# Dividing by exp(-ln) and a Newton step in a time mix, with the opening in another order

## The chip, the cores and the metric

One core of a Trainium2 chip runs one program; seven other cores are idle. The metric is the device time of that program in microseconds, the median of the runs of one kernel. The engines are TensorE (PE), VectorE (DVE), ScalarE (ACT), GpSimd (POOL), and the queue of DMA orders on SyncE (SP). Each engine works through its own instructions strictly in the order in which the program lists them; between engines, only semaphores order the work.

## The reference

Two layers of a gated model over x (16 sequences, 128 tokens, 256 channels) and a context of the same shape. Each layer is an attention-like part and a feed-forward part, each added to x through a gate `tanh(g)`:

```python
x = x + tanh(g_xattn[0]) * wkv(time_decay, time_first, layernorm(x), ctx)   # the time mix
x = x + tanh(g_ffn[0])   * ffn0(layernorm(x))       # gate/up/down MLP of 1024 and product-key experts
x = x + tanh(g_xattn[1]) * linear_attention(layernorm(x), ctx)
x = x + tanh(g_ffn[1])   * ffn1(layernorm(x))       # 8 routed experts, top 2, and a shared one
```

The change is in the first line. Freed of its running maximum, the time mix is, per channel and over the tokens t of a sequence, with w = exp(-exp(time_decay)) and u = time_first:

```python
den_t = past_den + exp(u + k_t);            num_t = past_num + exp(u + k_t) * v_t
y_t = num_t / den_t
past_den = w * past_den + exp(k_t);         past_num = w * past_num + exp(k_t) * v_t
```

## The kernel before, in words

**Tiling.** The 16 sequences are handled as four groups of four (GT = 4), so that a group has 512 tokens. Activations of a group are kept transposed: 256 channels are two chunks (c = 0, 1) of 128 partitions, and a chunk is 128x512. The first layer's time mix is done by group g of `WKV_FIRST`, the feed-forwards by group f of `MAIN_FIRST`.

**One written order.** There is no planner at run time. `SCHED` is a list of steps (kind, group, part), made of `START`, of the feed-forward units with the steps that `PLAN` hangs behind each, and of `LAST`. Every engine runs through the same list and issues what it has to do in each step, so the list sets the order within each engine's queue. A feed-forward has 12 units (8 of gate and up, 4 of experts); part p of `mlp` is unit p-1, and the down matmuls follow three units later. TensorE writes into six PSUM banks, taken in turn; a bank is taken again only when its reader has freed it.

**The time mix of a group**, in steps: `wkv_in` 0 moments of x (VectorE; the reciprocal root on GpSimd, L1620 or L1625); 1 normalize (VectorE L1240, or ScalarE L1023 for the steps in `NORM_ACT`); 2 TensorE transposes (L649), ScalarE takes exp into the denominator rows (L1033), and GpSimd (parts 3 and 4; VectorE for the very first) multiplies by the context, v (L531). `wkv_out` 0 and 1: for each chunk VectorE scans the denominator and then the numerator (L1276). Parts 2 and 4: ScalarE scales the numerator's own term by exp(u) (L1039), GpSimd adds the past (L1649). The denominator's own term is treated so too in groups 0 and 1 (`DEN_SCALE`: L1009, L1644) and by one VectorE operation in groups 2 and 3 (L548). Parts 2 to 5: VectorE takes the reciprocal in two halves of 256 columns (L1288); parts 3 and 5: GpSimd multiplies (L1655). Parts 6 and 7: TensorE transposes back (L770), VectorE adds to x (L1244). `x_stats` follows with the new moments, and then `mlp_in`, whose normalize for feed-forward 0 is ScalarE's.

**Around it.** `kv_k` (TensorE L781) projects a tile of the context for the second layer's attention; `kv_e` (ScalarE L1047 to L1052: two relus, a copy, an exp) makes the keys; `kv_v` (TensorE L793) multiplies keys by values; `kv_c` (ScalarE L1056) copies the sum. `split` makes the high and low parts of a weight block (ScalarE L977, GpSimd L1590) and asks SP for the block two further on. `wq` does that for the query weights, `query` uses them. `mlp` is on TensorE L654 to L656 and L678, Silu on ScalarE (L1137), the product with up on VectorE (L1414). `peer_in` brings the routing tables over (VectorE L1385 for the low part), which TensorE spreads (L744).

ScalarE computes functions from a table; where the next function is not in the table that is loaded, the program has an ACT_TABLE_LOAD in front of it.

The lines that the change replaces, with who waits for whom:

```python
        else:                                   # VectorE, wkv_out 2 to 5
            c, half = divmod(part - 2, 2)
            den = by_token(ee_a[c][:, 1, :])[:, half * GT // 2:(half + 1) * GT // 2, :]
            ...
            last = dve.reciprocal(den, den)
            if half:
                last.then_inc(recip_ready, 1)
```

Of the kernel before, what the change touches and what calls it, by code (L numbers as in the profile page):

```python
# [256 lines left out]
def build(nc, io):  # L257
    with ExitStack() as ctx:
# [204 lines left out]
        scanned = sem("scanned")  # L463
# [2 lines left out]
        recip_ready = sem("recip_ready")
# [1399 lines left out]
```

## Time and profile before

| | us |
|---|---|
| median of 3 runs | 507.49 (507.08 to 510.03) |
| the profiled execution | 508.22, of which the span 506.4 |
| TensorE busy | 450.3 (89%) |
| VectorE busy | 347.2 (69%) |
| ScalarE busy | 247.2 (49%) |
| GpSimd busy | 173.8 (34%) |

The granted TensorE clock is 0.974 of full speed in the mean. The span is from the first instruction to the last; what lies around it is the difference to the program's own time. Busy times count only work: not waits, not branches or DMA orders. An engine's idle time costs something only where the end waits for it, so the table says that TensorE is near its bound over the whole, and the stretches and timelines must say where it is not.

### The profile page before, as it was taken

How to read it: one execution, taken by the hardware profiler on the slowest of the kernel's cores; microseconds unless marked ns; L12 is line 12 of the kernel's file. 1: busy time of each engine (PE TensorE's matmuls, PEld its weight loads, DVE VectorE, ACT ScalarE, POOL GpSimd, SP SyncE). 2: the span in 40 equal slices, each digit the busy share in tenths (PEclk: the TensorE clock that was granted, in tenths of full speed). 3: DMA queues.
4: the chain of work that ended last, by engine and by line, in shares of the span. 5: the costliest groups of instructions: out<-in, count | busy, mean ns of one | idle time of the engine just before them, and what ended most of it. 6: DMA issues, size and time to landing. Idle time of an engine off the chain costs nothing. (4 is left out here: it accounts for less than half of the span.)

```text
span 506.4 us, 7287 instructions
## 1 busy us (share of the span) xinstructions
PE 450.3 (89%) x2162; PEld 356.1 (70%) x2162; DVE 347.2 (69%) x994; ACT 247.2 (49%) x479; POOL 173.8 (34%) x181
## 2 busy tenths in 40 slices
PE   2769799589989999999999998998998899899991
PEld 1447588458668776888778786887776688788860
DVE  6968569988486964577978967888778354621173
ACT  2868264223577377455044416360751544955540
POOL 3787232354022333400000000060525015477771
PEclk9999799789999999999999999999999899999997
DMA  8421212002000000980000000142323223346494
GB/s 306 164 80 57 62 33 80 5 20 83 1 1 2 0 1 0 293 218 0 1 2 1 0 2 0 32 136 74 119 71 112 88 79 111 105 150 191 123 380 138
DMA packets 32966, 42.02 MB, mean 83 GB/s; under 512 B 3483, under 2 KB 26781, under 8 KB 32928
## 3 DMA queue, kind: packets, MB, share of 16 engines
q1 hardware_dynamic: 28224, 32.28, 21.0%
q0 software_dynamic: 3744, 8.42, 4.5%
q10 hardware_dynamic: 960, 0.86, 0.5%
q8 instruction: 19, 0.31, 0.3%
q14 instruction: 19, 0.16, 0.1%
HBM read 24.97 MB, written 18.39 MB: 86 GB/s over the span
## 5 line engine op out<-in xcount | busy, mean ns | idle before, releaser
L678 PE MATMUL acc<-w_down,act_s 128*128 128x256 f32 x384 | 91.5, 384 | 0.9 <-DVE act_s L1410 0.9
L678 PEld LDWEIGHTS acc<-w_down,act_s 128*128 128x128 f32 x384 | 73.6, 193 | 12.8 <-DVE act_s L1410 1.3
L654 PE MATMUL ring<-xt_h,up_l 128*128 128x512 f32 x160 | 71.1, 444 | 1.4 <-DVE kv_sum L1490 1.4
L1137 ACT ACTIVATE act_s<-ring 128x512 f32<-128x512 f32 x48 | 28.6, 596 | 73.5 <-PE ring L656 73.3
L655 PE MATMUL ring<-xt_l,up_h 128*128 128x512 f32 x160 | 63.4, 396 | 0.0
L656 PE MATMUL ring<-xt_h,up_h 128*128 128x512 f32 x160 | 63.3, 395 | 0.0
L1625 POOL TENSOR_TENSOR rstd<-var_eps,minus_half 128x4 f32<-128x4 f32 x14 | 14.5, 1039 | 135.7 <-DVE var_eps L1225 135.7
L717 PE MATMUL ring<-up_e,act_s 128*128 x184 | 45.7, 392 | 2.3 <-issue 2.0
L1677 POOL DMA_INDIRECT x_rows<-main_a,slots x32 | 31.1, 972 | 43.7 <-ACT main_a L1158 34.8
L1414 DVE TENSOR_TENSOR act_s<-ring,act_s 128x512 f32<-128x512 f32 x32 | 21.9, 686 | 34.3 <-ACT act_s L1137 16.4
L717 PEld LDWEIGHTS ring<-up_e,act_s 128*128 128x128 f32 x184 | 34.2, 196 | 7.2 <-issue 3.2
L654 PEld LDWEIGHTS ring<-xt_h,up_l 128*128 128x128 f32 x160 | 30.6, 191 | 9.3 <-issue 2.0
L649 PE MATMUL ring<-small,xn 128*128 128x128 f32 x144 | 20.7, 290 | 18.5 <-DVE xn L1240 13.6
L655 PEld LDWEIGHTS ring<-xt_l,up_h 128*128 128x128 f32 x160 | 30.5, 190 | 7.5 <-issue 1.9
L656 PEld LDWEIGHTS ring<-xt_h,up_h 128*128 128x128 f32 x160 | 30.2, 189 | 7.2
L649 PEld LDWEIGHTS ring<-small,xn 128*128 128x128 f32 x144 | 17.5, 149 | 22.0 <-issue 9.3
L1685 POOL DMA_INDIRECT y_rows<-act_s,block_home x16 | 16.3, 1019 | 31.7 <-ACT act_s L1195 27.1
L1218 DVE BATCH_NORM_STATS2 stats<-x_nat 128x6 f32<-128x256 f32 x64 | 22.4, 412 | 4.5 <-DMA x_nat<-in_x 4.2
L1244 DVE SCALAR_TENSOR_TENSOR x_nat<-ring,small,x_nat 128x512 f32<-128x512 f32 x24 | 18.0, 749 | 10.1 <-PE ring L918 7.7
L1137 ACT ACT_TABLE_LOAD x18 | 23.1, 1283 | 0.3
L1567 DVE TENSOR_TENSOR pairs<-ring,pairs 128x256 f32<-128x256 f32 x12 | 5.1, 424 | 25.4 <-ACT pairs L1178 25.4
L1288 DVE RECIPROCAL main_a<-main_a 128x256 f32<-128x256 f32 x12 | 20.0, 1715 | 0.1
(281 smaller groups left out, 1009.6 us busy)
## 6 DMA issues: line engine op xcount, KB each, us to landing
main_b<-x_rows SPq DMA_DIRECT2D x22, 257.0 KB, 3.0
x_rows<-v_t SPq DMA_DIRECT2D x1, 3983.5 KB, 16.1
up_l<-y_rows SPq DMA_DIRECT2D x5, 512.0 KB, 5.9
stage<-in_w_mlp SPq DMA_DIRECT2D x8, 256.0 KB, 2.6
up_e<-in_w_moe SPq DMA_DIRECT2D x8, 256.0 KB, 2.6
x_rows<-v_t SPq DMA_DIRECT2D x1, 1927.5 KB, 22.4
x_nat<-in_x SPq DMA_DIRECT2D x7, 256.0 KB, 7.9
out_x<-x_nat SPq DMA_DIRECT2D x6, 256.0 KB, 5.0
```

The costliest lines, as they stand in the source:

```text
L649: last = pe.transpose(bank[:, t * P:(t + 1) * P], xn[n % 2][:, t, c * P:(c + 1) * P], ident)
L654: pe.matmul(out, wl, xh, start=first, stop=False, skip_group_check=True)
L655: pe.matmul(out, wh, xl, start=False, stop=False, skip_group_check=True)
L656: return pe.matmul(out, wh, xh, start=False, stop=final, skip_group_check=True)
L678: last = pe.matmul(acc[t // 2][:, t % 2, :], act_s[n % RING][:, tok], w_down[:, u, :], start=u == 0 and t % 2 == 0, stop=final, skip_group ...
L717: last = pe.matmul(bank[:, j * 2 * P:(j + 1) * 2 * P], x_block_t[n % 2][:, c, j * P:(j + 1) * P], up_e[:, bass.ds(e * UP + c * 2 * P, 2 * ...
L1137: act.activation(act_s[n % RING][:, :], bank[:, :], ACT.Silu).then_inc(free_sem((step, "A", u)), 1)
L1218: last = dve.bn_stats(stats[:, n, t, :], x_nat[:, b, :])
L1244: return dve.scalar_tensor_tensor(out, bank, gates[:, gate:gate + 1], out, ALU.mult, ALU.add)
L1288: last = dve.reciprocal(den, den)
L1414: free((step, "B", u), dve.tensor_tensor(s[:, :], bank[:, :], s[:, :], ALU.mult))
L1677: pool.indirect_dma_start(x_rows[group_of(g)], bass.IndirectOffsetOnAxis(ap=slots[:, t, k:k + 1], axis=0), to_send[n % SENDS], None).then_ ...
```

## The change

A group's `wkv_out` is written anew. Denominators of both chunks are scanned first (part 0), the numerators after them (part 1). ScalarE scales the own term of both denominators and GpSimd adds the past, in all groups (part 2). The quotient is then made of a guess and one Newton step: ScalarE computes `guess = exp(-ln(den))` (part 3); VectorE multiplies `den * guess`, GpSimd `num * guess`; VectorE computes `(den * guess - 2) * (num * guess)`, which is the quotient with its sign turned (part 5). The sign is taken back by the gate, whose tanh is taken of -g. In part 4 the numerator's own term and past are added: by ScalarE and GpSimd as before, for group 0 by one VectorE operation (`NUM_DVE`).

`START` and the plans of feed-forwards 0 and 1 are reordered, and the normalize of group 2 goes from VectorE to ScalarE.

```diff
-START = """wkv_in 0 0, setup 0 0, wkv_in 0 1, wkv_in 1 0, wkv_in 0 2, kv_k 0 0, kv_e 0 0, wkv_out 0 0, wkv_in 1 1, kv_k 0 1,
-    wkv_out 0 1, wkv_in 1 2, wkv_out 0 2, kv_e 0 1, kv_v 0 0, kv_c 0 0, wkv_out 0 3 4, kv_k 0 2, kv_e 0 2, wkv_in 1 3,
-    wkv_out 0 5, kv_v 0 1, kv_c 0 1, wkv_in 1 4, split 0 0, kv_k 0 3, kv_e 0 3, kv_v 0 2, kv_c 0 2, wkv_out 1 0,
-    wkv_out 0 6 7, kv_k 1 0, kv_e 1 0, kv_v 0 3, kv_c 0 3, x_stats 0 0, split 0 1, wkv_out 1 1, kv_k 1 1, kv_e 1 1, kv_v 1 0,
-    kv_c 1 0, mlp_in 0 0 1, mlp_in 0 2, kv_v 1 1, kv_k 1 2, wq 0 0, wkv_out 1 2, kv_c 1 1, kv_e 1 2, wkv_out 1 3 4"""
+START = """wkv_in 0 0, setup 0 0, wkv_in 0 1, wkv_in 0 2, wkv_in 1 0, kv_k 0 0 1, wkv_out 0 0 2, wkv_out 0 1, kv_k 0 2, wkv_out 0 3 4,
+    wkv_in 1 1, wkv_out 0 5, kv_e 0 0, wkv_in 1 2, kv_e 0 1, kv_v 0 0, kv_c 0 0, kv_e 0 2, wkv_in 1 3 4, split 0 0, wkv_out 0 6 7,
+    kv_v 0 1, kv_c 0 1, kv_k 0 3, kv_e 0 3, x_stats 0 0, kv_v 0 2, kv_c 0 2, kv_k 1 0, wkv_out 1 0, kv_e 1 0, kv_v 0 3, kv_c 0 3,
+    split 0 1, wkv_out 1 1, kv_k 1 1, kv_v 1 0, kv_c 1 0, mlp_in 0 0 1, mlp_in 0 2, kv_k 1 2, kv_e 1 1, wkv_out 1 2, kv_v 1 1, kv_c 1 1,
+    kv_e 1 2, wkv_out 1 3 4, wq 0 0"""
 PLAN = {
     ("mlp", 0): {
-        3: "route_in 2 1, route_in 2 2, query 2 0, wkv_in 2 0",
-        4: "query 2 1, wkv_in 2 1, route 0 2 3, wkv_in 2 2 3 4",
+        3: "kv_k 1 3, route_in 2 1, route_in 2 2, kv_e 1 3, query 2 0, wkv_in 2 0",
+        4: "query 2 1, wkv_in 2 1, route 0 2 3, wkv_in 2 2 3 4, kv_v 1 3, kv_c 1 3",
...
-        7: "wkv_out 2 1",
-        8: "peer_in 0 0, wkv_out 2 2 3",
-        9: "wkv_out 2 4 5",
-        10: "wkv_out 2 6 7, x_stats 2 0, kv_k 1 3, kv_e 1 3",
-        11: "mlp_in 1 0, kv_v 1 3, kv_c 1 3, kv_m 0 0 1 2 3",
+        7: "wkv_out 2 2",
+        8: "peer_in 0 0, wkv_out 2 1, kv_k 2 0 1",
+        9: "wkv_out 2 3 4 5, kv_e 2 0 1",
+        10: "wkv_out 2 6 7, x_stats 2 0, kv_v 2 0 1, kv_c 2 0 1",
+        11: "mlp_in 1 0, kv_m 0 0 1 2 3",
...
     ("mlp", 1): {
-        1: "mlp_out 0 0, route 1 4, kv_k 2 0, kv_e 2 0",
-        2: "route 1 5, kv_k 2 1, kv_v 2 0, kv_c 2 0, kv_e 2 1",
-        3: "route 1 6, wkv_in 3 0, kv_k 2 2, kv_v 2 1, kv_c 2 1, kv_e 2 2",
-        4: "route 1 7, wkv_in 3 1, kv_k 2 3, kv_v 2 2, kv_c 2 2, kv_e 2 3",
-        5: "wkv_in 3 2 3 4, route 1 8, kv_v 2 3, kv_c 2 3",
-        6: "wkv_out 3 0 1",
-        7: "wkv_out 3 2 3",
-        8: "peer_in 1 0, wkv_out 3 4 5, query 1 0",
+        1: "mlp_out 0 0, route 1 4",
+        2: "route 1 5, kv_k 2 2, kv_e 2 2",
+        3: "route 1 6, wkv_in 3 0, kv_k 2 3, kv_v 2 2, kv_c 2 2, kv_e 2 3",
+        4: "route 1 7, wkv_in 3 1, kv_v 2 3, kv_c 2 3",
+        5: "wkv_in 3 2 3 4, route 1 8",
+        6: "wkv_out 3 0 2 1",
+        7: "wkv_out 3 3 4",
+        8: "wkv_out 3 5, peer_in 1 0, query 1 0",
...
-DEN_SCALE = {(0, 0): 0, (0, 1): 1, (1, 0): 0, (1, 1): 2}
-
-NORM_ACT = {("wkv_in", 1), ("mlp_in", 0)}
+NUM_DVE = (0,)
+
+NORM_ACT = {("wkv_in", 1), ("wkv_in", 2), ("mlp_in", 0)}
...
-            act.activation(gates, gates, ACT.Tanh).then_inc(act_setup, 1)
+            act.activation(gates[:, 0:1], gates[:, 0:1], ACT.Tanh, scale=-1.0)
+            act.activation(gates[:, 1:], gates[:, 1:], ACT.Tanh).then_inc(act_setup, 1)
...
+                elif kind == "wkv_out" and part == 2:
+                    for c in range(C):
+                        act.wait_ge(den_scanned, C * g + c + 1)
...
+                        den = by_token(ee_a[c][:, 1, :])
+                        act.activation(den, den, ACT.Copy, scale=own_weight[:, c:c + 1]).then_inc(den_scaled, 1)
+                elif kind == "wkv_out" and part == 3:
+                    for c in range(C):
+                        guess = past_of(g, c, 1)
+                        act.wait_ge(den_ready, C * g + c + 1)
+                        act.activation(guess, by_token(ee_a[c][:, 1, :]), ACT.Ln).then_inc(den_log, 1)
+                        act.wait_ge(den_log, C * g + c + 1)
+                        act.activation(guess, guess, ACT.Exp, scale=-1.0).then_inc(guess_ready, 1)
...
+                elif kind == "wkv_out" and part == 5:
+                    for c in range(C):
+                        den = by_token(ee_a[c][:, 1, :])
+                        dve.wait_ge(guess_ready, C * g + c + 1)
+                        last = dve.tensor_tensor(den, den, past_of(g, c, 1), ALU.mult)
+                    link(last)
+                    for c in range(C):
+                        y = by_token(ee_a[c][:, 0, :])
+                        dve.wait_ge(guess_applied, C * g + c + 1)
+                        dve.scalar_tensor_tensor(y, by_token(ee_a[c][:, 1, :]), 2.0, y, ALU.subtract,
+                                                 ALU.mult).then_inc(y_ready, 1)
...
+                elif kind == "wkv_out" and part == 5:
+                    for c in range(C):
+                        y = by_token(ee_a[c][:, 0, :])
+                        pool.wait_ge(guess_ready, C * g + c + 1)
+                        pool.wait_ge(past_added, C * g + c + 1)
+                        pool.tensor_tensor(y, y, past_of(g, c, 1), ALU.mult).then_inc(guess_applied, 1)
```

## Rows read from the trace of the kernel before

**Rows 1.** page: busy time of each engine, its share of the span, its instructions.

```profile
PE 450.3 (89%) x2162; PEld 356.1 (70%) x2162; DVE 347.2 (69%) x994; ACT 247.2 (49%) x479; POOL 173.8 (34%) x181
```

**Rows 2.** by stretch: length; busy PE, PEld, DVE, ACT, POOL; PEclk; DMA share; GB/s.

```profile
0.00:40.00 40.00, 22.74 (x106) 15.01 (x107) 30.44 (x56) 23.34 (x58) 25.76 (x35) 1.00 0.53 182
...
90.00:110.00 20.00, 12.42 (x41) 8.90 (x41) 19.48 (x21) 3.62 (x7) 8.68 (x6) 0.79 0.00 1
...
140.00:170.00 30.00, 28.48 (x131) 22.36 (x130) 23.91 (x42) 18.46 (x28) 7.05 (x7) 1.00 0.00 1
```

**Rows 3.** timeline, VectorE, opening: start us, duration us, then instruction and releaser.

```profile
11.93 6.57 DVE L1276 TENSOR_TENSOR_SCAN main_b<-decay,main_a 128x516 f32<-128x516 f32 x4
18.42 6.55 DVE L1288 RECIPROCAL main_a<-main_a 128x256 f32<-128x256 f32 x4
24.90 1.16 DVE L1276 TENSOR_TENSOR_SCAN q_pad<-decay,xt_f_pad 128x516 f32<-128x516 f32 x1
27.07 2.28 DVE L1276 TENSOR_TENSOR_SCAN q_pad<-decay,xt_f_pad 128x516 f32<-128x516 f32 x1 [1.01 <-POOL xt_f_pad L531]
```

**Rows 4.** timeline, GpSimd, opening.

```profile
11.23 1.54 POOL L1620 TENSOR_TENSOR rstd<-var_eps,minus_half 128x4 f32<-128x4 f32 x1 [3.57 <-DVE var_eps L1225]
...
13.11 2.15 POOL L531 TENSOR_TENSOR main_a<-main_a,v_t 128x512 f32<-128x512 f32 x1
15.70 1.71 POOL L1644 TENSOR_TENSOR main_a<-main_a,main_b 128x512 f32<-128x512 f32 x1 [0.44 <-ACT main_a L1009]
```

**Rows 5.** timeline of all engines, up to the first feed-forward matmuls.

```profile
28.32 1.09 PE L770 MATMUL ring<-small,main_a 128*128 128x128 f32 x8 [2.28 <-POOL main_a L1655]
...
31.16 0.39 ACT L1047 ACTIVATE k_e<-ring 128x256 f32<-128x256 f32 x1 [1.06 <-PE ring L781]
...
31.89 1.88 PE L781 MATMUL ring<-wkv,v_odd 128*128 128x512 f32 x4
...
31.97 0.43 ACT L1052 ACTIVATE k_e<-k_e 128x256 f32<-128x256 f32 x1
...
33.61 0.40 PE L793 MATMUL ring<-v_x,k_e 128*128 128x136 f32 x2
...
35.26 2.07 ACT L1023 ACTIVATE xn<-x_nat,shift,rstd 128x256 f32<-128x256 f32 x4
...
40.56 0.80 PE L654 MATMUL ring<-xt_h,up_l 128*128 128x512 f32 x1
...
43.75 0.40 PE L654 MATMUL ring<-xt_h,wq_l 128*128 128x512 f32 x1
...
44.32 0.60 ACT L1137 ACTIVATE act_s<-ring 128x512 f32<-128x512 f32 x1
```

**Rows 6.** timeline, TensorE, around the third time mix: its two waits.

```profile
95.47 0.77 PE L744 MATMUL ring<-exps_t_l,sel_exps 128*128 128x512 f32 x1 [5.44 <-DVE exps_t_l L1385]
...
107.43 1.21 PE L770 MATMUL ring<-small,main_a 128*128 128x128 f32 x8 [2.15 <-POOL main_a L1655]
```

**Rows 7.** the groups by line and shape: busy us, mean ns of one, idle before.

```profile
L1288 DVE RECIPROCAL main_a<-main_a 128x256 f32<-128x256 f32 x12 | 20.0, 1715 | 0.1
...
L1410 DVE TENSOR_TENSOR act_s<-act_s,host_s 128x512 f32<-128x512 f32 x16 | 11.5, 721 | 6.0 <-ACT act_s L1137 5.6
...
L1039 ACT ACTIVATE main_a<-main_a,own_weight 128x512 f32<-128x512 f32 x6 | 4.3, 722 | 1.2 <-DVE main_b L1276 1.2
```

**Rows 8.** timeline, ScalarE: what stands around two table loads in the feed-forward.

```profile
151.96 1.28 ACT L1052 ACT_TABLE_LOAD   x1
153.26 0.42 ACT L1052 ACTIVATE k_e<-k_e 128x256 f32<-128x256 f32 x1
153.69 1.28 ACT L1137 ACT_TABLE_LOAD   x1
```

**Rows 9.** timeline, ScalarE: its first functions, behind one table load at 1.77.

```profile
5.30 0.20 ACT L995 ACTIVATE small<-small 128x4 f32<-128x4 f32 x1 [2.24 <-DMA small<-in_small]
5.41 0.19 ACT L996 ACTIVATE ew<-small 128x2 f32<-128x2 f32 x1
```

More of the change, by code:

```diff
@@ L462, in build @@
         first_values = sem("first_values")
[L463 removed]
         own_scaled = sem("own_scaled")
         past_added = sem("past_added")
[L466 removed]
+        den_scanned = sem("den_scanned")
+        num_scanned = sem("num_scanned")
         den_scaled = sem("den_scaled")
+        den_log = sem("den_log")
+        guess_ready = sem("guess_ready")
+        guess_applied = sem("guess_applied")
         den_ready = sem("den_ready")
@@ L1003, in _ @@
                 ee_a, ee_b = ee_a_of[g], ee_b_of[g]
-                if kind == "wkv_out":
-                    for c in range(C):
-                        if DEN_SCALE.get((g, c)) == part:
-                            act.wait_ge(scanned, C * g + c + 1)
-                            den = by_token(ee_a[c][:, 1, :])
-                            act.activation(den, den, ACT.Copy, scale=own_weight[:, c:c + 1]).then_inc(den_scaled, 1)
                 if APPLY.get(kind) == part and step in NORM_ACT:
@@ L1034, in _ @@
                                        bias=bias_a[:, c:c + 1]).then_inc(free_sem((step, "T", c)), 1)
-                elif kind == "wkv_out" and part in (2, 4):
-                    c = part // 2 - 1
-                    act.wait_ge(scanned, C * g + c + 1)
-                    own = by_token(ee_a[c][:, 0, :])
-                    act.activation(own, own, ACT.Copy, scale=own_weight[:, c:c + 1]).then_inc(own_scaled, 1)
+                elif kind == "wkv_out" and part == 2:
+                    for c in range(C):
+                        act.wait_ge(den_scanned, C * g + c + 1)
+                        if g == 0 and c == 0:
+                            act.wait_ge(first_values, 1)
+                        else:
+                            act.wait_ge(ev_ready, C * g + c)
+                        den = by_token(ee_a[c][:, 1, :])
[7 more added lines that the diff above has]
+                        act.activation(guess, guess, ACT.Exp, scale=-1.0).then_inc(guess_ready, 1)
+                elif kind == "wkv_out" and part == 4 and g not in NUM_DVE:
+                    for c in range(C):
+                        act.wait_ge(num_scanned, C * g + c + 1)
+                        own = by_token(ee_a[c][:, 0, :])
+                        act.activation(own, own, ACT.Copy, scale=own_weight[:, c:c + 1]).then_inc(own_scaled, 1)
                 elif kind == "kv_e":
@@ L1268, in _ @@
                     normalize(step, seqs)
[L1269 to L1271 removed]
+                elif kind == "wkv_out" and part == 0:
+                    if g == 0:
+                        weigh_values(dve, 0, 0).then_inc(first_values, 1)
+                    for c in range(C):
                         freed(dve, (("wkv_in", g), "T", c))
[L1273 to L1294 removed]
@@ new lines, in _ @@
+                        dve.tensor_tensor_scan(ee_b[c][:, 1, :], decay[:, c, :], ee_a[c][:, 1, :], 0.0, ALU.mult,
+                                               ALU.add).then_inc(den_scanned, 1)
+                elif kind == "wkv_out" and part == 1:
+                    if g == 0:
+                        dve.wait_ge(first_values, 1)
+                    for c in range(C):
+                        if g > 0 or c > 0:
+                            dve.wait_ge(ev_ready, C * g + c)
+                        dve.tensor_tensor_scan(ee_b[c][:, 0, :], decay[:, c, :], ee_a[c][:, 0, :], 0.0, ALU.mult,
+                                               ALU.add).then_inc(num_scanned, 1)
+                elif kind == "wkv_out" and part == 4 and g in NUM_DVE:
+                    for c in range(C):
+                        dve.wait_ge(num_scanned, C * g + c + 1)
+                        add_past(dve, g, c, 0).then_inc(past_added, 1)
+                elif kind == "wkv_out" and part == 5:
+                    for c in range(C):
+                        den = by_token(ee_a[c][:, 1, :])
+                        dve.wait_ge(guess_ready, C * g + c + 1)
+                        last = dve.tensor_tensor(den, den, past_of(g, c, 1), ALU.mult)
+                    link(last)
+                    for c in range(C):
+                        y = by_token(ee_a[c][:, 0, :])
+                        dve.wait_ge(guess_applied, C * g + c + 1)
+                        dve.scalar_tensor_tensor(y, by_token(ee_a[c][:, 1, :]), 2.0, y, ALU.subtract,
+                                                 ALU.mult).then_inc(y_ready, 1)
+                elif kind == "wkv_out" and part >= 6:
```

47 lines of the change are left out of this document (8 added, 39 removed).

## The prediction

> **What bounds the kernel now.** The page's busy times come first: TensorE 450.3 of 506.4 us, ScalarE under half [rows 1]. So time is lost where TensorE stands idle, and the stretches show where: 17.3 us before 40, 7.6 us between 90 and 110 (there VectorE is busy 19.5 of 20 us, ScalarE 3.6, and the granted clock is 0.79), and 1.5 us between 140 and 170 [rows 2]. The timelines then name the chains. In the opening, the time mix of group 0 runs scans, reciprocals, GpSimd's product, TensorE's transposes at 28.32; after them residual, moments, ScalarE's normalize at 35.26, the first gate matmul at 40.56, the query matmul at 43.75, the first Silu at 44.32 [rows 3 to 5]. Around 100, TensorE waits 5.44 us for VectorE's split of the expert table, which is queued behind group 2's scans, and 2.15 us for the mix's result [rows 6]. The change touches both stretches.
>
> **What VectorE gets back.** A 512-wide reciprocal is two of 1.715 us; sixteen halves cost 27.4 us [rows 7]. In their place a chunk has one product and one scalar-tensor-tensor at 0.72 us each [rows 7], 1.44 us for 3.43. Eight chunks: 16 us less. The additions of the past move off VectorE in groups 2 and 3 and onto it in group 0, which nearly cancels. Bounds for the two new operations: 0.72 us alone and twice that when GpSimd works beside them, as one scan took 2.28 us beside a product and 1.16 alone [rows 3]; at the upper end they still cost less than the reciprocals. I count 0.8.
>
> **What ScalarE gets.** Per chunk a Ln and an Exp over 512 columns. The same size took 0.60 as Silu and 0.72 as scaled copy [rows 5, 7]; I take 0.65. The trace has no Ln, so its table is the unknown. Lower bound: no load (the end at which Ln and Exp share the table that is there). Upper bound: a load of 1.283 us at each change, four for the two chunks of a group, because the loop runs Ln, Exp, Ln, Exp. Where Exp stands between two Silus the trace has a load on either side of it [rows 8]: the program loads for the next instruction and does not keep both. That row is the nearest, so I take four, and a fifth in groups 2 and 3 for the way back to Silu; group 2's keys share that return and save one pair. Group cost: 4 x 1.28 + 4 x 0.65 = 7.7 us in ScalarE's queue. A load's whole price is its 1.28 us: load at 151.96, Exp at 153.26, next load at 153.69, 0.01 to 0.02 us apart [rows 8]. The Trainium skill ("ScalarE: Activation LUTs", What ACT_TABLE_LOAD costs) adds a drain of about 1.38 us, 2.66 us a switch; by that the seven loads exposed in the opening would cost 9.7 us more. By that rule the rows would stand 1.4 us further apart; the trace disagrees and its number is used.
>
> **Opening, group 0.** Exps end at 11.96. From 11.93 VectorE scans both denominators, 1.16 and 2.28 us beside GpSimd's product of values [rows 3]: 15.4. GpSimd: that product to 14.1, then group 1's reciprocal root, 1.54 + 0.31, which now stands behind it: 16.0; additions 1.71 and 1.3 [rows 4]: 17.7 and 19.0. ScalarE's scalings lie beside this. Its first load is done while it waits, as the load at 1.77 was, long before the wait that ended at 5.30 [rows 9]. Ln 0: 18.4, load, Exp 20.4, load, Ln 22.3, load, Exp 24.3. GpSimd's product 1.3 and VectorE's last step end at about 27, a good 1 us before the 28.3 of now [rows 5]. But queued behind the last Exp is group 1's normalize, 2.07 us: 26.4; then keys of tile 0, 1.24 us (31.16 to 32.40 [rows 5]): 27.6. TensorE's queue waits for both, so its transposes of the mix come no earlier than 28.6. It is behind by what it did between 17.6 and 27 in the old order. Up to the feed-forward's transposes it still owes: mix transposes 1.1, five keys-by-values of 1.0 (eight matmuls, the first two in 0.40 at 33.61), three projections of 1.88 [rows 5]: 11.7 us, with 1.4 us of short waits for ScalarE: 40.7. Copy 0.4, normalize 2.07, transposes 1.1: 44.3. Projection 1.9, keys-by-values 1.0: the gate starts at 47.2, not 40.56: **+6.6**.
>
> **Group 1 and the query.** ScalarE from 44.9: two keys steps, two scalings, one copy: 4.3; the Ln and Exp chain, nothing hidden, 7.7; two more scalings 1.4; the high half of Wq 0.4: 58.7. This last cast was ahead of the chain and is now behind it, and TensorE's query matmul waits for its low half (GpSimd 0.73): 59.6 against 43.75 [rows 5], **+15.9** in all, with the same TensorE work done. Silu follows its load at 60.0 against 44.32. TensorE has only one unit's 2.8 us of work in between.
>
> **First feed-forward, group 2.** The stretch 90 to 110 has 7.6 us of TensorE idle [rows 2]. The change puts two projections and two keys-by-values there, 2 x 1.88 + 2 x 0.5 = 4.7 us that come out of the next, full unit: **-4.7**. Against it: denominators are summed at about 95, ScalarE ends its chain 7.7 us after the Silu of unit 8 at about 105, its own-weight scalings 106.5, GpSimd 109, result 109.9 for 107.4; then keys and load, so unit 9's Silu comes at about 111. With six banks and three a unit TensorE runs two units ahead: **+2.7**. Group 1's last tile moves from unit 10 to unit 3: same work, no net. With it move four transfers in SP's queue (group 3's context in two, Wqg, Wo), which wait for that tile's projection and now stand ahead of a weight block. Blocks are asked for two units, some 7 us, ahead, so I count nothing; without that lead, 3 us. The six other moved steps in this plan have their operands early and are counted at nothing; their cover is TensorE's own matmuls, and each uncovered would cost under 1.9 us. The normalize of group 2 on ScalarE (2.07 us, 1.4 on VectorE) falls at unit 4, where both engines have slack. The split Tanh is one more activation of 0.2 us [rows 9], under the wait for group 0's statistics: nothing.
>
> **Second feed-forward, group 3.** In unit 6 ScalarE's chain is five loads, two Ln, two Exp, two scalings: 6.4 + 2.6 + 1.4 = 10.4 us between two Silus. TensorE has two units of gate and up, about 7 us, before its banks are all held: **+3.4**. VectorE was not the bound there: TensorE busy 28.5 of 30 [rows 2].
>
> **Sum:** 15.9 - 4.7 + 2.7 + 3.4 = +17.3 on the profiled 508.2 us (span 506.4 and 1.8 around it): 525.5. This execution is 0.7 us above the median of the three runs, 507.49, inside their spread of 3; I forecast 525.
>
> **Rivals.** (B) *Ln and Exp share one table.* The Trainium skill says so ("ScalarE: Activation LUTs", Table sets: the hidden batching unit): one set holds both, so Ln then Exp is one load. Worked out from rows as a mechanism: one load a visit at most. Group 0 loses three exposed loads (3.85), group 1 all four (5.1), group 2 three (with its stall of 2.7 gone), group 3 three (its stall of 3.4 gone): 17.3 - 8.9 - 6.1 = +2.3, 510 us; the hidden steps above, if uncovered, make that 508 to 515, and I put it at 511. For it: Tanh and Exp do share a table, with nothing loaded between 5.30 and 5.41 [rows 9]. Against it: Silu and Exp do not, and the program went back and forth 3 us for one Exp [rows 8]. (C) *VectorE's relief decides,* faster: the place is 90 to 110, where VectorE is the bound. Its queue loses 6.9 - 3.2 us of reciprocals for quotient steps, two additions (1.6) and two scans ahead of the table split (2.4), so 7.6 idle us and the lowered clock can both go: about -8. It wins if the opening loses under 3 us, that is, if the guess for the second chunk of group 0 is out by 20.5 rather than 24.3 and ScalarE does not hold the query: 500 to 503. (D) *The gaps of the first 65 us bring the low clock.* Where TensorE idles now, from 90 to 110, the granted clock is 0.79 [rows 2], so part of that stretch is at the lower of its two levels, 1.2 for 2.4 GHz. A gap of 11 us before the query, then 8 us at the lower level, costs 4 us, with two more such places: 17.3 + 11 = 536. (E) The division might not leave the chain: two VectorE steps, each doubled by contention, plus GpSimd's are as long as a reciprocal pair; that changes only C's gain and is inside A.
>
> **Chances.** A 0.58 (519 to 532), B 0.20, C 0.14, D 0.08. One per cent, 5 us, is about what a measurement of this kernel can tell. Faster: C and a remnant of B, 0.15. Within 1%: half of B and the edge of A, 0.13. Slower: 0.72. The range, 511 to 537, leaves out C, the low part of B and the end of D.
>
> **What would show it.** ScalarE: 62 table loads for 46 (the groups by line, all together) and busy near 281 us for 247 [rows 1] (loads 20.5, Ln and Exp 10.4, four scalings of denominators less two of numerators 1.4, one normalize 2.1); under B some 48 loads. VectorE near 331 for 347. In the opening: the first guess near 20, the second near 24; gate near 47; query near 60 with TensorE idle for 10 us before it. Wrong would be: query before 50 (then B or C), TensorE without a wait between units 6 and 8 of the second feed-forward, or a result for group 2 before 107.

## The result, and the profile after

The changed kernel takes 539.78 us (median of 4 runs, 538.44 to 546.5) against 507.28 for the kernel before in the same job (505.56 to 510.03): 1.063 times as long, 95% interval 1.057 to 1.069. Medians are of all runs of a kernel; ratios leave out executions over 1.5% above its fastest, and hold each kernel against runs of the kernel before in its own job (their medians lie between 507.3 and 511.5). The forecast was 525, range 511 to 537. Its direction was right, its size half of what was measured: +17.3 us forecast, +32 measured.

The page's busy times, to be held against [rows 1]:

```profile
PE 452.6 (84%) x2162; PEld 359.2 (67%) x2162; DVE 334.9 (62%) x989; ACT 280.9 (52%) x518; POOL 177.4 (33%) x184
```

ScalarE has 33.7 us more work, as forecast (281), VectorE 12.3 us less. TensorE has the same work and a span of 538.1 us, so the 32 us are time in which it stands idle or is slow. By stretch (columns as in [rows 2]; the work of its 90 to 110 comes 20 us later here, so 110 to 130 is to be held against it; the rows from 198 on and the last one are about the clock):

```profile
0.00:40.00 40.00, 20.22 (x80) 13.64 (x81) 27.49 (x55) 24.03 (x50) 20.68 (x31) 0.87 0.50 172
40.00:65.00 25.00, 12.02 (x47) 8.74 (x47) 4.36 (x5) 21.16 (x38) 9.32 (x8) 0.72 0.06 18
110.00:130.00 20.00, 11.48 (x38) 7.36 (x37) 9.59 (x12) 17.51 (x30) 9.26 (x9) 0.83 0.04 14
...
198.00:206.00 8.00, 3.03 (x7) 2.17 (x8) 5.88 (x8) 2.09 (x5) 2.40 (x2) 0.50 0.00 0
...
208.00:212.00 4.00, 4.00 (x19) 2.80 (x19) 0.00 (x0) 1.81 (x4) 0.00 (x0) 1.00 0.00 0
...
60.00:70.00 10.00, 7.48 (x26) 6.09 (x27) 6.81 (x6) 6.32 (x13) 7.81 (x7) 0.61 0.14 39
```

Between 40 and 65 ScalarE is busy 21.2 of 25 us and TensorE 12.0: the bound there is ScalarE now. Around group 2's mix VectorE is busy 9.6 of 20 us, where it had 19.5, and ScalarE 17.5, where it had 3.6. The timeline of ScalarE shows with what, in groups 0 and 1:

```profile
18.69 0.63 ACT L1046 ACTIVATE main_b<-main_a 128x512 f32<-128x512 f32 x1 [1.30 <-POOL main_a L1662]
19.34 1.28 ACT L1048 ACT_TABLE_LOAD   x1
20.63 0.63 ACT L1048 ACTIVATE main_b<-main_b 128x512 f32<-128x512 f32 x1
21.28 1.28 ACT L1046 ACT_TABLE_LOAD   x1
22.57 0.63 ACT L1046 ACTIVATE main_b<-main_a 128x512 f32<-128x512 f32 x1
23.22 1.28 ACT L1048 ACT_TABLE_LOAD   x1
24.51 0.63 ACT L1048 ACTIVATE main_b<-main_b 128x512 f32<-128x512 f32 x1
25.05 2.06 ACT L1021 ACTIVATE xn<-x_nat,shift,rstd 128x256 f32<-128x256 f32 x4
...
50.77 1.28 ACT L1046 ACT_TABLE_LOAD   x1
...
58.43 0.70 ACT L1053 ACTIVATE xt_f_pad<-xt_f_pad,own_weight 128x512 f32<-128x512 f32 x1
...
59.65 0.40 ACT L1081 ACTIVATE wq_h<-later 128x256 fp32r<-128x256 f32 x1
60.07 1.28 ACT L1151 ACT_TABLE_LOAD   x1
61.36 0.60 ACT L1151 ACTIVATE act_s<-ring 128x512 f32<-128x512 f32 x1
```

Ln (L1046) and Exp (L1048) never follow one another without a load, and the next activation here starts 0.01 us after a load's end (19.34 and 1.28 make 20.62, the Exp starts at 20.63). The second guess of group 0 ends at 25.1 (24.3 forecast), group 1's normalize comes behind it. What TensorE waits for, in its timeline:

```profile
27.16 1.97 PE L652 MATMUL ring<-small,xn 128*128 128x128 f32 x8 [9.60 <-ACT xn L1021]
...
43.77 1.82 PE L652 MATMUL ring<-small,xn 128*128 128x128 f32 x8 [2.44 <-ACT xn L1021]
...
62.52 0.77 PE L657 MATMUL ring<-xt_h,wq_l 128*128 128x512 f32 x1 [10.54 <-POOL wq_l L1678]
...
126.27 0.77 PE L657 MATMUL ring<-xt_h,up_l 128*128 128x512 f32 x1 [8.52 <-ACT v_x L1063]
...
202.97 0.77 PE L747 MATMUL ring<-exps_t_l,sel_exps 128*128 128x512 f32 x1 [7.94 <-DVE exps_t_l L1404]
...
205.27 3.15 PE L681 MATMUL acc<-w_down,act_s 128*128 128x256 f32 x8
```

Four waits of 8 to 11 us: group 1's normalize, the query weights' low half, banks held by projections whose keys stand behind group 2's Ln and Exp, and the expert table's split. The last had no wait in the kernel before. On VectorE it stands behind group 3's quotient (last four lines; the first four are group 1's):

```profile
62.72 1.66 DVE L1306 TENSOR_TENSOR xt_f_pad<-xt_f_pad,q_pad 128x512 f32<-128x512 f32 x1
64.30 1.76 DVE L1306 TENSOR_TENSOR er_pad<-er_pad,gate_pad 128x512 f32<-128x512 f32 x1
66.10 1.65 DVE L1311 SCALAR_TENSOR_TENSOR xt_f_pad<-xt_f_pad 128x512 f32<-128x512 f32 x1
67.67 0.68 DVE L1311 SCALAR_TENSOR_TENSOR er_pad<-er_pad 128x512 f32<-128x512 f32 x1
...
197.53 0.69 DVE L1433 TENSOR_TENSOR act_s<-ring,act_s 128x512 f32<-128x512 f32 x1 [7.29 <-ACT act_s L1151]
198.25 2.69 DVE L1306 TENSOR_TENSOR main_a<-main_a,main_b 128x512 f32<-128x512 f32 x2
200.98 1.29 DVE L1311 SCALAR_TENSOR_TENSOR main_a<-main_a 128x512 f32<-128x512 f32 x2
202.19 0.68 DVE L1404 TENSOR_TENSOR exps_t_l<-ring,exps_t_h 73x512 fp32r<-73x512 f32 x1
```

The split needs 0.68 us and comes 4.7 us after the product that is ahead of the four quotient steps (202.19 less 197.53). That product itself waited 7.3 us for a Silu behind ScalarE's chain.

**A table by stage** reads every kernel below but e16: the start of a Silu in three places (unit 4 of the first feed-forward; unit 4 of the second; unit 0 of the third), less the same Silu of the kernel before (73.6, 155.0, 210.3). The first column is what the opening and group 1 lost, the second what the stretch with group 2 added, the third what group 3 added. Each is of one profiled execution, and where the program is the same up to the place that is read, such columns still differ: e8 and e9 have -0.7 and 1.2 in the first, e12 and e17 have -7.7 and -4.7 in the second. A difference under 3 us in the first two columns is no finding.

| kernel | opening, group 1 | group 2 | group 3 | together | median, us | ratio (95%) |
|---|---|---|---|---|---|---|
| forecast | +15.9 | -2.0 | +3.4 | +17.3 | 525 | |
| after the change | +20.6 | -1.6 | +12.9 | +32.0 | 539.8 | 1.063 (1.057 to 1.069) |
| e1, no Ln | +11.0 | -5.7 | +9.1 | +14.5 | 524.3 | 1.029 (1.025 to 1.034) |
| e2, loads halved | +15.9 | -4.0 | +11.6 | +23.4 | 533.6 | 1.047 (1.041 to 1.052) |
| e3, wq first | +22.0 | -0.4 | +14.5 | +36.1 | 546.8 | 1.071 (1.064 to 1.078) |
| e4, table first | +19.2 | -1.6 | +9.4 | +26.9 | 536.7 | 1.056 (1.050 to 1.062) |
| e7, e2 and e4 | +16.6 | -5.1 | +4.4 | +15.9 | 525.0 | 1.033 (1.023 to 1.042) |
| e18, e7 and keys first | +14.5 | -4.2 | +5.3 | +15.6 | 522.8 | 1.021 (1.017 to 1.025) |
| e5, new order, reciprocals | +14.0 | -4.8 | +9.1 | +18.2 | 526.4 | 1.032 (1.023 to 1.041) |
| e12, e5 and keys first | +7.9 | -7.7 | +9.1 | +9.3 | 521.8 | 1.028 (1.022 to 1.035) |
| e17, e12 and table first | +9.5 | -4.7 | +2.4 | +7.2 | 514.1 | 1.008 (1.004 to 1.013) |
| e6, old order, new division | +27.3 | +4.3 | +4.5 | +36.1 | 543.6 | 1.068 (1.059 to 1.077) |
| e10, old order, reciprocals | +13.9 | +1.2 | 0.0 | +15.1 | 524.4 | 1.032 (1.025 to 1.038) |
| e13, e10, reciprocals early | +10.6 | -3.3 | +3.9 | +11.2 | 520.3 | 1.022 (1.014 to 1.030) |
| e14, e13 by chunk | +9.7 | -5.8 | +3.8 | +7.7 | 516.9 | 1.012 (1.005 to 1.019) |
| e15, e14, sums early | +8.8 | -3.3 | +2.2 | +7.7 | 514.7 | 1.007 (1.001 to 1.012) |
| e8, before, new plans | -0.7 | -4.3 | +2.4 | -2.6 | 507.3 | 0.995 (0.991 to 1.000) |
| e11, e8, guess in group 2 | +1.6 | -5.8 | +3.2 | -0.9 | 509.4 | 0.999 (0.996 to 1.003) |
| e9, e8, group 2's sums moved | +1.2 | -8.5 | +2.7 | -4.7 | 502.7 | 0.989 (0.984 to 0.994) |

### The profile page after: what moved, and what is told of

It reads as the page before. It is cut to its first block and busy times, and to the rows that moved or that the text cites. A ratio compares the mean times of both kernels' runs of the same rounds, so it can differ in the third digit from the quotient of the medians.

```text
span 538.1 us, 7331 instructions
## 1 busy us (share of the span) xinstructions
PE 452.6 (84%) x2162; PEld 359.2 (67%) x2162; DVE 334.9 (62%) x989; ACT 280.9 (52%) x518; POOL 177.4 (33%) x184
## 5 line engine op out<-in xcount | busy, mean ns | idle before, releaser
L681 PEld LDWEIGHTS acc<-w_down,act_s 128*128 128x128 f32 x384 | 73.4, 192 | 12.9 <-DVE act_s L1429 1.3
L658 PE MATMUL ring<-xt_l,up_h 128*128 128x512 f32 x160 | 64.6, 404 | 0.0
L659 PE MATMUL ring<-xt_h,up_h 128*128 128x512 f32 x160 | 64.5, 403 | 0.0
L1151 ACT ACTIVATE act_s<-ring 128x512 f32<-128x512 f32 x48 | 28.6, 596 | 68.7 <-PE ring L659 68.5
L720 PE MATMUL ring<-up_e,act_s 128*128 x184 | 44.2, 382 | 2.3 <-issue 2.1
L1695 POOL DMA_INDIRECT x_rows<-main_a,slots x32 | 31.1, 971 | 43.8 <-ACT main_a L1172 34.8
L720 PEld LDWEIGHTS ring<-up_e,act_s 128*128 128x128 f32 x184 | 33.1, 190 | 6.8 <-issue 3.2
L747 PE MATMUL ring<-exps_t_l,sel_exps 128*128 128x512 f32 x24 | 13.5, 564 | 8.8 <-DVE exps_t_l L1404 7.9
```

Of the source, the lines that this page charges most:

```text
L658: pe.matmul(out, wh, xl, start=False, stop=False, skip_group_check=True)
L659: return pe.matmul(out, wh, xh, start=False, stop=final, skip_group_check=True)
L681: last = pe.matmul(acc[t // 2][:, t % 2, :], act_s[n % RING][:, tok], w_down[:, u, :], start=u == 0 and t % 2 == 0, stop=final, skip_group ...
L720: last = pe.matmul(bank[:, j * 2 * P:(j + 1) * 2 * P], x_block_t[n % 2][:, c, j * P:(j + 1) * P], up_e[:, bass.ds(e * UP + c * 2 * P, 2 * ...
L1151: act.activation(act_s[n % RING][:, :], bank[:, :], ACT.Silu).then_inc(free_sem((step, "A", u)), 1)
L1695: pool.indirect_dma_start(x_rows[group_of(g)], bass.IndirectOffsetOnAxis(ap=slots[:, t, k:k + 1], axis=0), to_send[n % SENDS], None).then_ ...
```

## The experiments

**Are the table loads the loss?** e1 puts a Copy where the Ln stands; the quotient's values are thereby not the reference's, and every instruction but 14 loads stays.

```diff
-act.activation(guess, by_token(ee_a[c][:, 1, :]), ACT.Ln)
+act.activation(guess, by_token(ee_a[c][:, 1, :]), ACT.Copy)
```

> The changed kernel with Ln replaced by Copy, which needs no table of its own: 46 or 47 table loads for 62, every other instruction and the order kept (the quotient's values are left wrong). Theory 1, the table loads in ScalarE's queue are the main cost: 16 loads of 1.28 us go; about 9 us come back in the opening, 8 to 10 in the second feed-forward, some in the first: 517 to 524 us for 540. Rival, the new order costs most whatever the loads do: 530 to 536. If the opening recovers fully, the query matmul starts near 53 for 62.5.

524.3, at the upper edge of the first theory: half of the loss goes, half stays. TensorE's wait for the query weights is 5.1 us, down from 10.5 (its timeline):

```profile
53.54 0.77 PE L657 MATMUL ring<-xt_h,wq_l 128*128 128x512 f32 x1 [5.14 <-POOL wq_l L1678]
```

By stage the loads account for 9.6 us in the opening, 4.1 in group 2, 3.8 in group 3 (after less e1). The other 14.5 need another cause.

e2 takes both Ln first and then both Exp, so that a group has two loads in place of four:

```diff
 act.activation(guess, ..., ACT.Ln).then_inc(den_log, 1)
+for c in range(C):
     act.wait_ge(den_log, C * g + c + 1)
     act.activation(guess, guess, ACT.Exp, scale=-1.0)
```

> The changed kernel with part 3 as Ln, Ln, Exp, Exp: two loads a group instead of four, 54 for 62, same results. Theory 1: half of what the first run recovers, about 530 us, with VectorE's first product some 2.6 us later for chunk 0 and 2.6 us earlier for chunk 1. Rival: under 3 us gained, 537 or more.

533.6, where 530 was expected: 6.2 us less than after the change with 8 loads (10.3 us) fewer; most of it in the opening (4.7).

**Is it the order of single steps?** e3 moves `wq 0 0` from the end of the opening to before `wkv_out 1 2`; e4 swaps `wkv_out 3 5, peer_in 1 0` into `peer_in 1 0, wkv_out 3 5`.

> The changed kernel with the step wq 0 0 ahead of group 1's wkv_out 2 instead of behind its parts 3 and 4. Theory 1 with the cast as the wait that ends last: the 10.54 us in which TensorE waits at the query matmul go, and the time falls by 8 to 10 us, to 531. Rival, the first Silu at 61.4 is the real limit and the banks fill a unit later: 0 to 4 us, 536 to 540.

> The changed kernel with peer_in 1 0 ahead of wkv_out 3 5 in part 8 of the second feed-forward. VectorE splits the expert table before the quotient steps of group 3. Theory: the 7.94 us wait of TensorE and the clock at its lower level after it shrink, 530 to 534 us. Rival, TensorE then waits as long for ScalarE, whose Silu of unit 7 ends at 197.4: 536 to 539.

e3 gains nothing, against both expectations: 546.8 for 539.8, with intervals that overlap. The wait for the query goes, and TensorE then stands 13 us for group 1's result:

```profile
68.10 0.47 PE L773 MATMUL ring<-small,xt_f_pad 128*128 128x128 f32 x1 [13.08 <-DVE er_pad L1311]
```

So the cast's place sets where TensorE waits and not what it loses: group 1's chain is as late behind it. e4 takes 536.7, what its rival expected, and gives 3.5 us back in its stage. e7 has the edits of e2 and e4:

> Two edits together on the changed kernel: Ln, Ln, Exp, Exp, and peer_in 1 0 ahead of wkv_out 3 5. Apart they took 6 and 3 us off. If the wait at the table of group 3 is one chain, they share it and give 8 together or less, 532; if they are separate places, 9 or more, 530.

525.0, less than either expectation. In group 3 batching alone gives 1.3 us, the swap alone 3.5, both together 8.5. The waits at the expert table (TensorE's timelines of e4 and e7, and the stretch behind each) say why:

```profile
197.88 0.76 PE L747 MATMUL ring<-exps_t_l,sel_exps 128*128 128x512 f32 x1 [4.36 <-DVE exps_t_l L1404]
197.90:201.00 3.10, 3.10 (x7) 2.15 (x8) 3.06 (x5) 0.66 (x2) 0.52 (x1) 0.50 0.00 0
...
189.29 0.47 PE L747 MATMUL ring<-exps_t_l,sel_exps 128*128 128x512 f32 x1 [1.75 <-DVE exps_t_l L1406]
189.30:192.00 2.70, 2.70 (x11) 2.16 (x13) 2.67 (x3) 0.66 (x2) 2.23 (x1) 1.00 0.00 0
```

The wait is 7.94 us after the change, 5.37 in e2, 4.36 in e4 and 1.75 in e7: batching takes 2.6 off, the swap 3.6, both 6.2. ScalarE's chain and VectorE's quotient steps stand one behind the other, and their savings add up. What comes on top is the clock: behind the waits of after, e2 and e4 the granted clock is 0.50, behind e7's it is 1.00. From the wait's end to the Silu of unit 9 it is 11.7, 12.0, 11.8 and, in e7, 9.4 us, which puts the price of the low clock at about 2.3 us there.

**Which half is the order's, which the division's?** e5 has the new order and, in part 5, the four reciprocals in place of the guess, its product and the last step; e6 has the new division in the `START` and `PLAN` of before.

> The changed kernel's order, but the quotient by VectorE's reciprocals as before: in part 5 VectorE takes the reciprocal in two halves a chunk and GpSimd multiplies; no Ln, no Exp, 46 table loads, Tanh of the gates unsplit. Theory 1 (ScalarE's queue, loads and functions): most of the 32 us go, since the copies-for-Ln run at 524 still had 10 us of Ln and Exp in that queue; 511 to 518. Rival, the order is what costs: 524 or more.

> The new division (Ln, Exp and Newton step, denominators scanned first, normalize of group 2 on ScalarE) with START and PLAN of the kernel before. Theory 1: the four loads a group cost the same in any order, 525 to 540. Rival, order: the old one puts keys and projections beside the chain and comes out at 507 to 518.

e5 loads no table for Ln and is still 3.2% slower than before, as its rival expected; e6 is 6.8% slower, 543.6 us, more than either of its expectations. Neither half alone is the loss. TensorE's timeline of e5:

```profile
28.65 1.97 PE L773 MATMUL ring<-small,main_a 128*128 128x128 f32 x8 [7.86 <-POOL main_a L1661]
...
43.55 1.55 PE L652 MATMUL ring<-small,xn 128*128 128x128 f32 x8 [2.44 <-ACT xn L1020]
```

The mix comes when it came before (28.32 in [rows 5]) and the feed-forward's transposes are as late as after the change (43.77). That delay needs neither Ln nor Exp. e10 undoes both, and keeps how the mix is worked: both chunks of a group in each part, the denominators' sums by ScalarE and GpSimd in all groups, group 0's numerators by VectorE, group 2's normalize on ScalarE.

> START and PLAN of before and VectorE's reciprocals, but with what else the change does to the mix: denominators of both chunks scanned first, both chunks finished together in part 5, VectorE adding group 0's numerators, normalize of group 2 on ScalarE. If the order of START is what costs 16 us in the run with the new order and the old division, this is within 4 us of before, 507 to 513. Rival, working both chunks together is what costs: 515 or more.

524.4: these four together cost 15 us, 13.9 of them before unit 4. That was the rival which my account had no term for. Three runs take the pairing apart, each with one edit more:

```diff
e13: -elif kind == "wkv_out" and part == 5:  # both chunks' reciprocals
     +elif kind == "wkv_out" and part == 3:
e14: -part 0: scan den 0, den 1      part 1: scan num 0, num 1
     +part 0: scan den 0, num 0      part 1: scan den 1, num 1
e15: -wkv_out 0 0, wkv_in 1 1, kv_k 0 1, wkv_out 0 1, wkv_in 1 2, wkv_out 0 2,
     +wkv_out 0 0 1 2, wkv_in 1 1, kv_k 0 1, wkv_in 1 2,
```

> The run before it in this line (order and reciprocals of the kernel before, both chunks of a group worked in pairs) took 524.4 us. Here one thing of it is changed: VectorE takes a group's reciprocals in part 3, as soon as the denominators are summed, and not in part 5 behind the numerators. Group 1's part 3 stands ahead of the first feed-forward unit, its part 5 behind that unit's product. If the pairing costs its 14 us because a group's reciprocals stand late in VectorE's queue: group 0's wait before them (2.4 us) and group 1's lag (7 us, of the Silus of units 0 to 4) go, and the time is 512 to 516. Rival, the pairing costs by the order of the scans and by GpSimd's sums of both chunks, which come after all scans wherever the reciprocals stand: 521 to 526.

> The kernel of the run with early reciprocals, and besides each chunk's two scans together, the first chunk's in part 0 and the second's in part 1, as in the kernel before; the own terms and sums of the denominators still come in pairs in part 2, in all groups. If scanning the denominators first matters (in either direction), it differs from the run with early reciprocals by over 3 us; the theory that only the reciprocals' place matters expects the same within 3 us. If both together undo the pairing's cost: 507 to 512.

> The kernel of the chunk-by-chunk run (516.9 us), with one thing changed: group 0's part 2, ScalarE's scaling of the denominators' own terms and GpSimd's sums, is put ahead of group 1's normalize (2.07 us), its two exps and the steps between in the opening's list. There the scaling ended at 20.0 and VectorE stood idle for 3.4 us ahead of its reciprocals at 20.75, where the kernel before has them at 18.42. If what the pairing still costs in the opening is where ScalarE's scaling stands in its queue: reciprocals near 18.5, the mix's transposes 2 us earlier than 31.9, the first Silu 2 us earlier than 52.1, time 513 to 515.5. Rival, the rest is in GpSimd's and ScalarE's own share of the work, or group 1's normalize, now late, takes the gain back: 516 to 519.

The ratio falls from 1.032 by 1.022 and 1.012 to 1.007; neighbours overlap in their intervals, the ends do not. So the pairing made most of e10's loss; how much each edit gives is less sure. VectorE's reciprocals in e10:

```profile
21.09 6.59 DVE L1299 RECIPROCAL main_a<-main_a 128x256 f32<-128x256 f32 x4 [2.41 <-POOL main_a L1650]
```

and in e15:

```profile
18.43 6.56 DVE L1297 RECIPROCAL main_a<-main_a 128x256 f32<-128x256 f32 x4
```

The first start is 2.7 us earlier, with no wait, as in [rows 3]: in e10 ScalarE's scaling of the denominators stood behind group 1's normalize. e13 expected too much (512 to 516; 520.3): it wins 7.8 us to the second stage and then loses 3.9 in group 3. e14 put the line at 3 us, and 3.4 came out, with intervals that overlap: whether the scans' order matters is not shown. e16 sums the denominators of groups 2 and 3 by one VectorE operation each, on top of e15:

> The kernel of the run with early sums, and besides the denominators of groups 2 and 3 summed by one VectorE operation each, as in the kernel before, in place of ScalarE's scaling and GpSimd's addition. If handing these sums to two engines costs (a chain of two engines for one operation, with VectorE waiting for it) it is 2 to 4 us faster than the run with early sums, 510 to 513, and the Silus behind unit 9 of the first and second feed-forward come closer to those of the kernel before. Rival, that part only moves work off VectorE and costs nothing: within 1 us of the run with early sums, or slower, as VectorE has 1.3 us more ahead of the expert table's split.

517.3, ratio 1.0105 (1.005 to 1.016) against 1.0065: no gain, so nothing says that handing these sums to two engines costs.

**The opening and group 3 of the new order.** e12 is e5 with TensorE's keys of group 0 (`kv_v 0 1, kv_k 0 3, kv_v 0 2`) ahead of `wkv_out 0 6 7`; e17 is e12 with e4's swap.

> The run with the new order and the old division, and in START two keys-by-values and one projection of group 0 stand ahead of the mix's transposes (wkv_out 0 6 7) instead of behind. TensorE idled 7.86 us at those transposes. If what it owes behind them sets the start of the feed-forward, 3.7 us come back, 521 to 523 for 526. Rival: the normalize behind the moments sets it: 525 to 527.

> The kernel of the run with the keys ahead of the mix (new order, reciprocals, no Ln and no Exp; profiled span 514.5, median 521.8), with one thing changed: in the second feed-forward's unit 8 the expert table's step stands ahead of wkv_out 3 5, so that VectorE splits the table before it takes group 3's reciprocals. There its Silu at the start of the third feed-forward was 9.2 us further behind the kernel before than the one in unit 4 of the second (219.7 less 210.3 against 155.2 less 155.0), with no table load in the kernel. If that step's place is the cause of what group 3 loses: at least 7 of the 9.2 us come back in this stage, TensorE's 3.9 us of idle time ahead of the table's spread is gone, and the time is 510 to 516. Rival, group 3 loses by both chunks' reciprocals being taken in one piece of VectorE's time, whatever stands ahead of them: the stage keeps over 5 of its 9.2 us and the time is 518 to 523.

e12's first gate matmul is at 42.7 and its first Silu at 47.3, where e5 has 48.7 and 53.4. Its opening loses 7.9 for 14.0, so the work put behind the mix was part of it. The size is less sure: e12's profile is of its fastest run and e5's of its slowest, e17 with the same opening loses 9.5, and the medians of e5 and e12 are too near for a verdict. e17 settles group 3: 9.1 us become 2.4, and the kernel 514.1, ratio 1.008 against 1.028. The 6.7 us are TensorE's wait of 3.9 us, which goes, and the clock behind it, 0.56 in e5 between 189 and 195. VectorE in e5, where the split waits:

```profile
181.77 6.59 DVE L1299 RECIPROCAL main_a<-main_a 128x256 f32<-128x256 f32 x4
188.28 0.62 DVE L1392 TENSOR_TENSOR exps_t_l<-ring,exps_t_h 73x512 fp32r<-73x512 f32 x1
```

and in e17, where it goes first and TensorE is busy without a break from 160 to 200:

```profile
178.84 0.69 DVE L1392 TENSOR_TENSOR exps_t_l<-ring,exps_t_h 73x512 fp32r<-73x512 f32 x1 [1.46 <-ACT exps_t_h L1135]
179.44 6.57 DVE L1299 RECIPROCAL main_a<-main_a 128x256 f32<-128x256 f32 x4
```

e18 puts e12's edit on e7, the new division at its best here:

> The new division in its best form from these runs: the kernel after the change, with its table loads halved (Ln, Ln, Exp, Exp), the expert table's step ahead of group 3's last steps (together 525.0), and besides keys of group 0 ahead of the mix's last steps in the opening. If TensorE's order in the opening still costs (with reciprocals this edit brought 5 us at the profiled runs' own times): 518 to 522. If the loads in ScalarE's queue set the opening now, the keys' steps are as late as the mix: 523 to 527. On neither theory does it reach the kernel before, 508.

522.8, still 2.1% slower than before.

**What is worth keeping.** e8 is the kernel before with the projections' and keys' steps moved in `PLAN` as in the change, and of the mix only group 2's second scans, which go behind the expert table's step; e9 adds one line; e11 has the new division, batched, in group 2 alone.

```diff
-DEN_SCALE = {(0, 0): 0, (0, 1): 1, (1, 0): 0, (1, 1): 2}
+DEN_SCALE = {(0, 0): 0, (0, 1): 1, (1, 0): 0, (1, 1): 2, (2, 0): 1, (2, 1): 2}
```

> The kernel before with its START and its division, and only the moved fillers: group 1's last tile at unit 3, two projections of group 2 and the expert table ahead of group 2's second chunk in part 8, keys behind them. Theory: TensorE's 7.6 idle us between 90 and 110 are filled with 4.7 us of work from the next, full feed-forward, and the table is split before the second chunk's scans: 500 to 504. Rival: TensorE then waits longer for the mix, 506 to 509.

> The kernel of the run plan_alone, and group 2's denominators are scaled by ScalarE (idle there) and added to by GpSimd instead of by one VectorE operation a chunk. If VectorE's queue holds the mix of group 2, its 2 us less bring TensorE's 4.21 us wait down and the time to 1 to 2 us under plan_alone, 503 to 506. Rival: GpSimd's addition beside a scan stretches both to 2.2 us and nothing is gained, 507 to 509.

> The kernel of the run plan_alone with the new division in group 2 alone, as Ln, Ln, Exp, Exp, where VectorE is busy 18.9 of 20 us and ScalarE 8.8: two loads more (the way back to Silu is shared with the keys). ScalarE's chain is 5.1 us, VectorE loses 6.9 us of reciprocals for about 3.5. Theory 1: in this place the division pays, the mix of group 2 comes some 2 us earlier: 503 to 506. Rival: the chain ends no earlier than the reciprocals did, 507 to 510.

e8 is at the edge of what can be told (-0.5%, what its rival expected); its second stage has 4.3 us less. e9 is faster than both kernels: 502.7, 1.1% under the one before, by an interval that leaves out 1. It gives group 2's denominator sums, which VectorE had in its fullest stretch, to ScalarE and GpSimd, which are idle there for over half of the time [rows 2]. TensorE's wait for group 2's result in e8:

```profile
106.04 1.97 PE L769 MATMUL ring<-small,main_a 128*128 128x128 f32 x8 [4.21 <-POOL main_a L1654]
```

and in e9:

```profile
105.94 1.09 PE L769 MATMUL ring<-small,main_a 128*128 128x128 f32 x8 [0.75 <-POOL main_a L1654]
```

e11 takes the reciprocals off VectorE in the one place where VectorE was the bound, and gains nothing over e8: 509.4, what its rival expected.

## Why the prediction was half right

**Right.** Four loads a group, 62 for 46: the groups by line of the kernel after hold them (L1046 and L1048 are Ln and Exp, L1151 Silu; in the last two rows the mean of the new VectorE steps):

```profile
L1151 ACT ACT_TABLE_LOAD x19 | 24.4, 1283 | 0.3
...
L1046 ACT ACT_TABLE_LOAD x8 | 10.3, 1283 | 0.1
L1048 ACT ACT_TABLE_LOAD x8 | 10.3, 1283 | 0.1
...
L1311 DVE SCALAR_TENSOR_TENSOR main_a<-main_a 128x512 f32<-128x512 f32 x6 | 6.3, 1097 | 3.9 <-POOL main_a L1673 3.8
L1306 DVE TENSOR_TENSOR main_a<-main_a,main_b 128x512 f32<-128x512 f32 x6 | 5.5, 923 | 8.7 <-ACT main_b L1048 8.6
```

Rival B (one table for both, 511 us) is refuted by the 16 loads at L1046 and L1048. The Trainium skill ("ScalarE: Activation LUTs", Table sets: the hidden batching unit) puts both functions in one set, so that Ln then Exp is one load; the trace disagrees for this program, with a load at every change, and e2 is 6 us faster with 8 of them fewer. Taking [rows 8] as the nearest row was the right choice. A load's price is its 1.28 us, as taken. The Trainium skill ("ScalarE: Activation LUTs", What ACT_TABLE_LOAD costs) has a drain of 1.38 us besides; the trace disagrees, with 0.02 us ahead of a load (18.69 and 0.63 make 19.32) and 0.01 behind it. The first feed-forward's -2.0 was -1.6, though with one wait of 8.52 us where the kernel before has 5.44 and 2.15 [rows 6]; its terms were not tested one by one, and part of the agreement may be luck. VectorE's new steps took 1.12 us in the mean (17.9 us for sixteen) where I counted 0.8; VectorE's busy time fell by 12.3 us, not 16.

**The opening: +15.9 forecast, +18.8 at the query, +20.6 by unit 4.** The sum has a slip: 28.6, 11.7 and 1.4 are 41.7, not 40.7; four keys-by-values follow the mix there, not five, and with four the 40.7 is right. The feed-forward's transposes came at 43.8 for 43.2, but the gate at 48.9 for 47.2: the granted clock is 0.72 in that stretch, and in e4, which has the same steps and 1.00 there, the gate is at 47.7. The query comes at 62.52 for 59.6. ScalarE's chain started 1.5 us later than I had it, and the low half of Wq waits in GpSimd's queue behind group 1's two additions, a queue which I had not looked at for this step. GpSimd's timeline:

```profile
59.21 1.27 POOL L1667 TENSOR_TENSOR xt_f_pad<-xt_f_pad,q_pad 128x512 f32<-128x512 f32 x1 [8.63 <-ACT xt_f_pad L1053]
60.43 1.26 POOL L1667 TENSOR_TENSOR er_pad<-er_pad,gate_pad 128x512 f32<-128x512 f32 x1
61.66 0.72 POOL L1678 TENSOR_TENSOR wq_l<-later,wq_h 128x256 fp32r<-128x256 f32 x1
```

Behind it group 1's quotient is made, and the granted clock is 0.61 between 60 and 70. I had closed the account at the query. The cause was half wrong too: I put it on ScalarE's chain, and e1, e5 and e10 lose 11 to 14 us of it without any Ln. Part of that is TensorE's work put behind the mix (e12), and in the old order part is that a group's parts wait for both chunks (e13 to e15 win back 5 of 13.9 us).

**Second feed-forward, group 3: +3.4 forecast, +12.9 measured. This step failed most.** It read: TensorE has two units of gate and up, about 7 us, before its banks are all held, and VectorE was not the bound there. The row that it names [rows 2] ends at 170, ahead of the place. The kernel before has there, on VectorE's timeline and by stretch:

```profile
172.30 0.69 DVE L1385 TENSOR_TENSOR exps_t_l<-ring,exps_t_h 73x512 fp32r<-73x512 f32 x1
...
170.00:180.00 10.00, 10.00 (x51) 7.74 (x50) 8.97 (x10) 5.30 (x10) 4.28 (x3) 1.00 0.00 0
```

The split stood between the two chunks' reciprocals, in a stretch in which VectorE is busy 9.0 of 10 us. The diff has `wkv_out 3 5, peer_in 1 0` where `peer_in 1 0` came first, and I did not price that swap; so a step which TensorE needs waits on VectorE for a quotient which waits on ScalarE. ScalarE's chain by itself was sized about right: with the swap taken back (e4) TensorE waits 4.4 us, for +3.4. After the change it waits 7.9. The low clock behind it costs about 2.3 more, which A left out: 0.50 between 198 and 206, and the down matmuls take 3.15 us where they took 1.89 before the gap. These make 10.2 of the 12.9 us; e8 and e17 lose 2.4 in this stage without such a wait. e5 has 9.1 us without Ln or Exp.

**The other rivals.** C (VectorE's relief decides) had the reciprocals gone and VectorE's busy time down, and it lost: e1 has that relief without the loads' price for Ln and is at 1.029, e11 has it in the very stretch and gains nothing. D (gaps bring the low clock) was inside the measured case: the mean granted clock is 0.947 for 0.974, and e3, with the longest gap, has 0.936. It was priced at 4 us a gap, about 2.3 in the one place where runs tell it apart, and given 0.08 as a case of its own; it belonged in A, since A's own gaps of 10 us were the condition for it. E (the new steps, stretched, are as long as the reciprocals) was nearly so: group 1's four VectorE steps run from 62.7 to 68.4, 5.6 us, and two chunks' reciprocals take 6.6.

**Open.** e15 starts its first Silu 3.5 us behind the kernel before and is 8.8 us behind in unit 4; what group 1 still loses there was not taken apart. Nor were the 2.4 us of group 3 in e8 and e17. Group 2's normalize on ScalarE and group 0's numerators on VectorE had no run of their own; both are in e15, which loses 0.7% in all.

## What to carry to other kernels

Before an approximation replaces a slow instruction, write down which table each of its functions needs in the order in which the loop issues them, and what stands behind the chain on that engine. Where an order of steps is rewritten, list every swap in which a step that the bounding engine waits for goes behind a step that waits on a third engine; each is a term of the sum, however small the step. Price a gap together with the clock behind it. Removing one wait proves nothing about its price (e3): another wait of the same length can stand behind it.

## What the runs showed of the hardware

- Two-input steps on VectorE stretch beside GpSimd's: L1306 and L1311 took 1.65 to 1.76 us between 62.7 and 67.7, with GpSimd at two-input steps of its own from 62.6 to 67.2, and 0.68 when it had finished. I had bounded them at twice 0.72; it was up to 2.4 times. GpSimd's two products took 1.72 us there, and the shortest of that kind in this trace 1.27, so both pay.
- The clock came down in a gap and stayed down for the work behind it: TensorE idle from 195.0 to 203.0, granted 0.50 from 198 to 206, that is 1.2 of 2.4 GHz, and 1.00 again from 208 on. So a gap of 8 us was followed by matmuls at the lower clock, 3.15 us for 1.89. At the same step e2 and e4, with gaps of 5.4 and 4.4 us, have 0.50 behind them, and e7, with 1.75 us, has 1.00.
